# Row sums of the 64-wide attentions: halves added on GpSimd, one spread product, weights through buffers of their own

## The reference

```
qkv = layernorm/modulate(x) @ W_qkv;  q, k, v = split
(L3a only: q and k are normalised per head over their 64 features)
attn = softmax(q k^T / 8);  out = attn v
x = x + [gate *] (out @ W_out [+ bias])
```

## Time and profile before

| | us |
|---|---|
| median of 3 runs | 3928.55 (3927.75 to 3930.52) |
| the profiled execution | 3926.93 |
| its span | 3925.1 |

### The profile page before, as it was taken

One profiled execution on the slowest core, in us unless ns is written; L12 is line 12 of the kernel. 1 busy time (PEld: TensorE's weight loads), 2 busy tenths in 40 slices (PEclk: granted clock), 3 DMA queues, 4 the chain that ended last, 5 costly groups with the idle time before them and its releaser, 6 DMA issues. The chain is left out here.

```text
span 3925.1 us, 74223 instructions
## 1 busy us (share of the span) xinstructions
PE 3291.2 (84%) x27690; PEld 2698.3 (69%) x27690; DVE 2291.2 (58%) x4337; ACT 1729.5 (44%) x3098; POOL 513.8 (13%) x519
## 2 busy tenths in 40 slices
PE   4999999997978869899997894999989899843686
PEld 2777777776977759777776783666666666632576
DVE  3555665555656656567775565565565655446464
ACT  1444344434533225445553553566565655400353
POOL 0000000000101001212232110110101101010243
PEclk8999999998988879999998996999999999855798
DMA  4000000001000000100000101000000000110243
GB/s 144 4 5 5 5 5 3 5 6 36 21 25 0 0 23 0 42 19 0 0 0 0 39 21 51 1 0 0 0 0 0 0 0 0 61 50 0 68 114 66
DMA packets 63631, 80.65 MB, mean 21 GB/s; under 512 B 9570, under 2 KB 56546, under 8 KB 63284
## 3 DMA queue, kind: packets, MB, share of 16 engines
q1 hardware_dynamic: 57412, 71.13, 6.1%
q0 software_dynamic: 6144, 8.52, 1.1%
HBM read 66.80 MB, written 12.85 MB: 20 GB/s over the span
## 5 line engine op out<-in xcount | busy, mean ns | idle before, releaser
L1431 ACT ACTIVATE L0a_prob<-L0a_st 128x512 f32<-128x512 f32 x256 | 138.7, 597 | 180.4 <-PE L0a_st L1638 180.4
L1431 ACT ACTIVATE L3a_prob<-L3a_st 128x512 f32<-128x512 f32 x256 | 138.8, 597 | 145.4 <-PE L3a_st L1638 145.4
L1881 DVE TENSOR_REDUCE L0a_mx<-L0a_s 128x2 f32<-128x512 f32 x256 | 164.7, 685 | 53.4 <-PE L0a_s L1614 48.1
L1881 DVE TENSOR_REDUCE L3a_mx<-L3a_s 128x2 f32<-128x512 f32 x256 | 164.5, 684 | 38.1 <-PE L3a_s L1614 36.6
L2174 ACT ACTIVATE L2a_prob<-L2a_st 128x512 f32<-128x512 f32 x256 | 132.3, 604 | 117.4 <-PE L2a_st L2214 117.4
L1359 POOL TENSOR_TENSOR L3a_shift<-L3a_neg,L3a_mx 128x256 fp32r<-128x256 f32 x128 | 87.3, 682 | 699.2 <-DVE L3a_mx L1881 699.2
L2451 DVE TENSOR_REDUCE L2a_mx<-L2a_s 128x2 fp32r<-128x512 f32 x256 | 163.5, 681 | 15.5 <-PE L2a_s L2214 15.5
L1860 DVE TENSOR_TENSOR L0a_qk_lo<-L0a_st,L0a_qk_hi 128x512 fp32r<-128x512 f32 x128 | 87.5, 691 | 88.1 <-ACT L0a_qk_hi L1395 88.1
L1871 DVE SCALAR_TENSOR_TENSOR L3a_qk_lo<-L3a_raw,cols_sb,L3a_qk_hi 128x256 fp32r<-128x256 f32 x256 | 124.6, 537 | 19.1 <-ACT L3a_qk_hi L1422 18.6
L3138 ACT ACTIVATE moe_xt<-moe_xm 128x1024 fp32r<-128x1024 f32 x8 | 8.5, 1056 | 277.8 <-DVE moe_xm L3235 277.8
L1669 PE MATMUL L3a_o<-L3a_prob,L3a_v 128*64 128x256 f32 x1024 | 124.6, 385 | 0.0
(11 more groups left out here) (607 smaller groups left out, 11988.1 us busy)
## 6 DMA issues: line engine op xcount, KB each, us to landing
moe_stage<-in_moe_w SPq DMA_DIRECT2D x16, 1024.0 KB, 5.9
...
```

Source lines behind the costliest of these rows:

```text
L1431: A(prob[:, u % 4, h, :], st_ps[u % 2][h][:], ACT.Exp, scale=64 ** -0.5).then_inc(p_done, 1)
L1881: V.tensor_reduce(mx[:, u % 2, h, :], s_ps[h][:].rearrange("p (t n) -> p t n", t=TT), AX.X, ALU.max).then_inc(mx_done, 1)
```

## The change

In both attentions:

1. Row sums. After column_part(p) of pairs 0, 1 and 2, POOL adds the second half of the keys' exponentials to the first, in place (`halves`), and PE sums only the 4 matmuls of the first half (`sums(p, True)`). Pair 3 keeps its 8 (`sums(3, False)`). sums(0) and sums(1) stand inside row_part(2) and row_part(3), ahead of the second half of the subtractions; sums(3) stands between column_part(2) and column_part(3), and sums(2) ends the sample.
2. Spread. The selector makes the sums twice, in rows 0 to 3 and 4 to 7 of each group of 32; ACT rounds with a sign and DVE forms high part and remainder in one tile (`rsum_both`), so `over` is one matmul for each half.
3. Order. next_norm stands behind over(1) (L3a) or over(0) (L0a); in L3a project(0), qk(6), the o_high of ACT, modulate and the qn_low of DVE move too, and take(i-1) of DVE moves behind the next maxima.
4. Weights. q and k come as eight pieces of 128x512 in buffers of their own, all loaded at once; v has two buffers, its remainder is formed by POOL; the output weights are loaded in two pieces through one buffer, the second once the first is done, and both are rounded and split by POOL behind its work on sample 0. PE begins with four pieces done, and both PE and DVE wait for the output weights (`wo_done`) ahead of sample 1.

```diff
-        for w_dram, dst in ((t[nm + "_wq"], wq), (t[nm + "_wk"], wk), (t[nm + "_wv"], wv)):
-            for k in range(KD):
-                pieces.append((w_dram[k * P:(k + 1) * P, :], dst[0][:, k, :], dst[1][:, k, :], qknorm and dst is not wv))
-        for c in range(0, U, 4):
-            pieces.append((t[nm + "_wo"][c * P:(c + 4) * P, :].rearrange("(c p) n -> p c n", p=P),
-                           wo[0][:, c:c + 4, :], wo[1][:, c:c + 4, :], False))
...
+        for half in range(2):
+            for j, (name, w) in enumerate((("_wq", wq), ("_wk", wk))):
+                for k in range(KD):
+                    at = slice(512 * half, 512 * half + 512)
+                    pieces.append((t[nm + name][k * P:(k + 1) * P, at], v[:, j, 512 * k:512 * k + 512] if half else prob[:, j, k, :],
+                                   w[0][:, k, at], w[1][:, k, at]))
+        o_stage = o32[:].rearrange("p a n -> p (a n)")
+        v_stage = [prob[:, 3, :, :].rearrange("p h n -> p (h n)"), o_stage]
...
             for q in range(4):
-                sp.dma_start(spread32[32 * q:32 * q + PAIRS, :], by_sum[q]).then_inc(spread_in, 16)
+                for low in range(2):
+                    at_row = 32 * q + PAIRS * low
+                    sp.dma_start(spread32[at_row:at_row + PAIRS, :], by_sum[q]).then_inc(spread_in, 16)
...
+            for n in range(2):
+                if n:
+                    sp.wait_ge(wo_done, 1)
+                else:
+                    sp.wait_ge(wv_done, 2)
+                sp.dma_start(o_stage.rearrange("p (c n) -> p c n", n=D),
+                             t[nm + "_wo"][4 * n * P:4 * (n + 1) * P, :].rearrange("(c p) n -> p c n", p=P)).then_inc(o_landed[n], 16)
...
+            for k in range(KD):
+                gated_wait(wv_hi, k + 1)
+                nc.gpsimd.tensor_tensor(wv[1][:, k, :], v_stage[k], wv[0][:, k, :].bitcast(F32), ALU.subtract).then_inc(wv_done, 1)
+
+            def output_weights():
+
+                for n in range(2):
+                    src, cs = o_stage.rearrange("p (c n) -> p c n", n=D), slice(4 * n, 4 * n + 4)
+                    gated_wait(o_landed[n], 16)
+                    nc.gpsimd.tensor_copy(wo[0][:, cs, :], src).then_inc(wo_hi, 1)
+                    gated_wait(wo_hi, n + 1)
+                    nc.gpsimd.tensor_tensor(wo[1][:, cs, :], src, wo[0][:, cs, :].bitcast(F32), ALU.subtract).then_inc(wo_done, 1)
+
+            def halves(i, p):
+
+                gated_wait(pv_done, PAIRS * i + p + 1)
+                both = prob[:, 2 * p % 4:2 * p % 4 + 2, :, :]
+                nc.gpsimd.tensor_tensor(both[:, :, :, 0:N], both[:, :, :, 0:N], both[:, :, :, N:2 * N], ALU.add).then_inc(halves_done, 1)
+
             if qknorm:
-                gated_wait(made, 2 + PAIRS)
-                def shifts(i):
...
+                def body(i):
+                    for u in range(6):
+                        shift_of(i, u)
+                    halves(i, 0)
+                    shift_of(i, 6)
+                    shift_of(i, 7)
+                    halves(i, 1)
+                    halves(i, 2)
+
...
             else:
...
+                def body(i):
+                    tail(i)
+                    for p in range(3):
+                        halves(i, p)
+
+                token_rstd(1)
+                body(0)
+                output_weights()
+                with pool.Fori(1, B - 1) as i:
                     token_rstd(i + 1)
-                    tail(i)
-                tail(B - 1)
...
                 act.wait_ge(rsum_done, j + 1)
-                A(rsum_hi[:], rsum[:], ACT.Copy).then_inc(rsum_hi_done, 1)
+                A(rsum_hi[:], rsum[:], ACT.Identity, scale=sign[:]).then_inc(rsum_hi_done, 1)
...
-                    if c >= 4 and not first:
+                    if qknorm and c >= 3 and c < 7 and not first:
+                        o_high(i - 1, c - 3)
+                    if not qknorm and c >= 4 and not first:
...
-                    mm(bank[:, h * N:(h + 1) * N], spread[:, c * P:(c + 1) * P], rsum_hi[:], start=True, stop=False)
-                    last = mm(bank[:, h * N:(h + 1) * N], spread[:, c * P:(c + 1) * P], rsum_lo[:], start=False, stop=True)
+                    last = mm(bank[:, h * N:(h + 1) * N], spread[:, c * P:(c + 1) * P], rsum_both[:], start=True, stop=True)
...
+                    if p >= 2:
+                        sums(p - 2, True)
...
+
+                def sums(p, halved):
+
+                    if halved:
+                        pe.wait_ge(halves_done, 3 * i + p + 1)
+                    else:
+                        pe.wait_ge(p_done, 2 * (U * i + 2 * p) + 4)
+                    for kt in range(1 if halved else TT):
                         for odd in range(2):
                             for h in range(2):
                                 at = 64 * odd + 32 * h
                                 last = mm(sum_ps[at:at + 32, 0:N], sum_sel[:, p, :],
                                           prob[:, (2 * p + odd) % 4, h, kt * N:(kt + 1) * N],
-                                          start=(p == 0 and kt == 0), stop=(p == PAIRS - 1 and kt == TT - 1),
-                                          skip_group_check=True)
-                    if p == PAIRS - 1:
+                                          start=(p == 0), stop=(p == 2), skip_group_check=True)
+                    if p == 2:
                         last.then_inc(sums_done, 1)
...
                     qk(0)
                     qk(1)
-                    next_norm()
                     qk(2)
                     last_over(0)
                     qk(3)
                     last_over(1)
+                    next_norm()
                     qk(4)
+                    last_project(0)
                     variances(0)
                     variances(1)
-                    last_project(0)
                     last_over(2)
                     qk(5)
                     last_over(3)
+                    qk(6)
                     qk_scale(0)
-                    qk(6)
                     last_project(1)
                     qk_scale(1)
                     qk(7)
                     qk_scale(2)
                     variances(2)
                     if first:
-                        pe.wait_ge(lo_done, 3 * KD)
...
+                        if c == 4:
+                            next_norm()
...
                     row_part(p)
                     column_part(p - 1)
-                column_part(PAIRS - 1)
+                sums(3, False)
+                column_part(3)
...
-            pe.wait_ge(made, 2 + PAIRS)
-            pe.wait_ge(lo_done, 2 * KD)
-            if qknorm:
-                pe.wait_ge(spread_done, 1)
+            pe.wait_ge(made, 2 + 2 * PAIRS)
+            pe.wait_ge(lo_done, 4)
             body(0, True, False)
             pe.wait_ge(spread_done, 1)
-            pe.wait_ge(lo_done, len(pieces))
+            pe.wait_ge(wo_done, 2)
             with pe.Fori(1, B - 1) as i:
                 body(i, False, False)
...
-                V.tensor_tensor(rsum_lo[:], rsum[:], rsum_hi[:].bitcast(F32), ALU.subtract).then_inc(rsum_lo_done, 1)
+                V.scalar_tensor_tensor(rsum_both[:], rsum[:], low_row[:], rsum_hi[:].bitcast(F32), ALU.mult, ALU.add).then_inc(both_done, 1)
...
-                    row_low(i - 1)
+                    row_both(i - 1)
                 if not final:
                     normalise(i + 1)
                 if qknorm:
+                    last_over(0)
+                    last_over(1)
                     if not final:
                         modulate(i + 1)
-                    last_over(0)
-                    last_over(1)
                     last_o_low(0)
                     last_over(2)
                     last_o_low(1)
...
                     rq_low(1)
-                    qn_low(2)
                     maxes(1)
                     for u in range(4, U):
                         qk_scaled(u)
-                    qn_low(3)
                 else:
                     qk_low(1)
...
+                    if p + 1 < PAIRS:
+                        maxes(2 * p + 2)
                     if p == 0 and not first:
                         take(i - 1)
                     if p + 1 < PAIRS:
-                        maxes(2 * p + 2)
                         maxes(2 * p + 3)
-                    if qknorm and p < 2:
-                        qn_low(2 * p + 4)
-                        qn_low(2 * p + 5)
+                    if qknorm and p < 3:
+                        qn_low(2 * p + 2)
+                        qn_low(2 * p + 3)
...
+            dve.wait_ge(wo_done, 2)
```

97 lines of the change are left out of this document (69 added, 28 removed).

## The result

The changed kernel takes 4078.8 us (median of 4 runs, 4076.9 to 4083.2), the kernel before 3929.5 beside it (median of 4): ratio 1.0378, 95% interval 1.036 to 1.0396. It is slower by 149 us, where 103 were forecast. The forecast of 4030 us was 49 too low, 46 of them in the difference; the time lies in the range of 3970 to 4085, near its upper end.

What follows compares the result with a forecast made beforehand. PE was taken to set the end in both attentions, with few gaps. The terms 150 - 39 - 13 - 18 + 22 + 2 - 1 gave +103 us on the profiled 3926.93, so 4030 us was predicted; range 3970 to 4085.

Steps and rivals of the forecast that it cites:

- The stall in L0a: L0a: PE waits 6.95 us a steady sample for halves(0) inside row_part(2); net of the saved sums +6.45 us.
- the forecast chain: L0a, POOL: tail waits for the gate rows, then runs 1.28 us, then halves(0) takes 2.42 us while PE waits.
- Rival (b): L0a: halves(0) meets PE in time, so 15 x 9.35 = 140 us go: 3890 us; chance 8%.
- The clock in L0a: L0a: PE at 1.2 GHz for some 5 us after each stall, costing 2.4 us a sample, bounds 1.6 and 2.9.
- Rival (a): The stall is there but the clock stays up: -36 in L0a, -5 at the output weights, 3989 us; chance 10%.
- Spread, pairs 1 to 3, end in L0a: L0a, a steady sample: +0.25 us for the spread, +0.15 for pairs 1 to 3, +0.75 at the sample's end.
- L3a: L3a: a steady sample gains 2.6 us, bounds -4.0 and -1.0; -39 us over 15 samples.
- pair 2: L3a, pair 2: DVE leads with qn_low of units 4 and 5, the sum's 0.5 us not gained, 0.3 lost.
- Before the first sample: Earlier start from loading weights at once: -13 us in L0a (bounds -6, -18), -18 us in L3a (bounds -12, -20).
- Output weights: Both attentions: PE and DVE wait 8.7 us, clock falls again (2.4): +11 us each, +22, bounds 15 and 28.
- Rival (c): L0a and L3a: POOL's additions are slower on this layout, say 4 us: about 4105 us; chance 9%.

Runs made afterwards that it cites:

- experiment 1: The changed kernel, but in L0a GpSimd runs its three additions of halves ahead of tail(i) instead of behind it: 3957.2 us.
- experiment 4: The changed kernel, but in L3a PE sums pair 0 in full and GpSimd adds no halves for it: 4048.0 us.
- experiment 3: The kernel before, with an added stage of VectorE instruction rows beside one GpSimd addition or copy: 3977.7 us in one execution.
- experiment 5: The changed kernel, but in L3a VectorE takes qn_low at the places of the kernel before, GpSimd's addition kept: 4095.7 us.

## Why the prediction was right in sign and 46 us short

- **The stall in L0a: right.** 6.95 us of wait forecast, 6.3 to 6.7 measured, by the forecast chain; net of the time saved 6.45 forecast and 6.2 measured (62.1 - 54.1 us between after and experiment 1, less 1.8 of clock); halves(0) took 2.34 us, not the 2.82 of the upper bound. Experiment 1 took it away. Rival (b) had no case.
- **The clock in L0a: right in kind, near in size by luck.** 2.4 us a sample forecast, 3.1 measured: 1.8 behind the stall, less than forecast for it, and 1.3 behind the wait for o_low(0), which the forecast did not price. Rival (a) falls.
- **Spread, pairs 1 to 3, end in L0a: right within 0.2 us each.** Forecast 0.25, 0.15 and 0.75. Measured in experiment 1, from the start of a sample to project(0) 12.28 us against 12.00, in pairs 1 to 3 0.05 and 0.28, from column_part(2) to the end 4.63 against 3.81. In the forecast's 0.25 the wait for o_low(0) more than doubled (0.9 to 2.2 us) without changing the sum; that is what the clock answered to. 6.2 + 0.3 + 0.2 (a new wait of PE for DVE's gated output, line 1923) + 0.3 + 0.8 + 3.1 = 10.9 us a sample, the measured difference of the periods.
- **L3a: the step that failed.** Forecast -4.1 at the front, +0.3 in pair 2, +0.45 in pair 3, +0.75 at the end: -2.6 (bounds -4.0 and -1.0). Measured in one sample, from its start to column_part(0) 40.96 us against 44.92 (-3.96), on to (1) 7.89 against 5.56 (+2.33), on to (2) 5.62 against 5.29 (+0.33), the end +0.82, and the slow stretch of 3.4 us in every third sample, half of it lost, +0.6: +0.1 in all; the windows have +0.2. So one term was mis-sized, pair 2 (+2.33 for +0.3), and one was missing, the clock (+0.6); experiment 4, without that addition, has it at 1.00. L3a lies outside its own bounds; the total stayed in its range because the range was wide. The forecast did see that halves(0) runs beside qn_low, and priced it by the 0.4 us between two durations of POOL's addition (met twice in each of 15 samples that makes 12 us, not the 6 that it says). Those two show what POOL lost to DVE in other stages. What DVE loses to POOL is nearly the whole addition, 2.1 us, and it sat on PE's path in every sample. Experiments 3, 4 and 5 show it.
- **Before the first sample: right.** ACT reached qk_hi(0) at 77.01 us (80.5 forecast, 93.55 before). Of the two stretches of the table the first is 5 us better than forecast and the second 2 us worse. The terms given for L3a add to 2403.7 us and not 2402.8, which changes nothing.
- **Output weights: the wait right, its worth 6 us too high.** 8.7 us forecast, 9.20 and 9.3 measured; without them 15.8 us less instead of 22. In L0a:

```profile
125.56 1.04 POOL L1377 CAST L0a_wo<-L0a_o 128x1024 fp32r<-128x1024 f32 x1 [3.95 <-DMA L0a_o<-in_L0a_wo]
126.77 2.34 POOL L1379 TENSOR_TENSOR L0a_wo<-L0a_o,L0a_wo 128x1024 fp32r<-128x1024 f32 x1 [0.18 <-POOL L0a_wo L1377]
...
129.45 0.57 PE L1574 MATMUL L0a_st<-L0a_xt,L0a_wq 128*128 128x256 f32 x1 [9.20 <-POOL L0a_wo L1379]
```

The second piece is cast 3.95 us after the first was done, when its load has landed, and PE's first projection of sample 1 starts as the last subtraction ends.

- **Rival (c), slower additions on this layout: wrong.** They take 2.34 to 2.50 us.
